# A rebuilt front of an expert layer: the gate turned round, the sort done with bf16 flags, three of four normalisations on GpSimd

## What is computed

```python
def _L0_ffn_ref(x, Wg, bg, W1, b1, W2, b2):     # x: the normalised rows
    x_flat = x.reshape(N * T, d)
    logits = x_flat @ Wg + bg
    probs = jax.nn.softmax(logits, axis=-1)
    assignments = jnp.argmax(probs, axis=-1)
    h = jnp.einsum('nd,edh->neh', x_flat, W1) + b1[None]
    h = jax.nn.gelu(h, approximate=False)
    eo = jnp.einsum('neh,ehd->ned', h, W2) + b2[None]
    selected = jnp.take_along_axis(eo, assignments[:, None, None], axis=1)[:, 0, :]
    w = jnp.take_along_axis(probs, assignments[:, None], axis=1)
    out = (w * selected).reshape(N, T, d)
x = x + _L0_ffn_ref(_layernorm(x, axis=-1), ...)
```

## Time and profile before

| | us |
|---|---|
| median of 3 runs | 2192.9 (2190.82 to 2194.61) |
| the profiled execution, whole | 2189.86 |
| its span, first to last instruction | 2187.2 |

### The profile page before, as it was taken

One profiled execution on the slowest core, in us unless ns is written; L12 is line 12 of the kernel. 1 busy time (PEld: TensorE's weight loads), 2 busy tenths in 40 slices (PEclk: granted clock), 3 DMA queues, 4 the chain that ended last, 5 costly groups with the idle time before them and its releaser, 6 DMA issues. The chain is left out here.

```text
span 2187.2 us, 34853 instructions
## 1 busy us (share of the span) xinstructions
PE 1982.6 (91%) x10933; PEld 1395.2 (64%) x10933; DVE 1400.2 (64%) x2902; ACT 1150.3 (53%) x2171; POOL 989.6 (45%) x1035
## 2 busy tenths in 40 slices
PE   4899999999999838899999999999999587799997
PEld 3667666677666425556565656565655286688896
DVE  4666657666565435767676767676766234688886
ACT  3555555455555422555555555555554243378785
POOL 2356555555564641444444444444444211255544
PEclk9999999999999768999999999999999855899999
DMA  5334353443434243333333334343423256222220
GB/s 154 88 92 130 104 143 104 121 136 94 135 100 104 87 164 83 73 88 102 92 102 93 102 93 102 93 102 93 102 69 88 88 187 230 58 85 80 87 85 24
DMA packets 129135, 227.27 MB, mean 104 GB/s; under 512 B 26362, under 2 KB 27426, under 8 KB 128992
## 3 DMA queue, kind: packets, MB, share of 16 engines
q1 hardware_dynamic: 110640, 194.97, 32.2%
q0 software_dynamic: 12704, 29.44, 4.9%
q10 hardware_dynamic: 5648, 1.07, 0.3%
HBM read 94.82 MB, written 37.24 MB: 60 GB/s over the span
## 5 line engine op out<-in xcount | busy, mean ns | idle before, releaser
L390 POOL TENSOR_TENSOR cross_probs<-cross_probs 128x1024 f32<-128x1024 f32 x128 | 305.2, 2388 | 361.4 <-ACT cross_probs L492 361.3
L590 DVE TENSOR_REDUCE cross_m_col<-cross_sS 128x1 f32<-128x512 f32 x512 | 340.1, 685 | 188.6 <-PE cross_sS L743 185.2
L492 ACT ACTIVATE cross_probs<-cross_sT 128x512 f32<-128x512 f32 x512 | 305.3, 598 | 266.9 <-PE cross_sT L759 261.9
L593 DVE CUSTOM_DVE_ANT_0 self_sS<-self_sS,self_tri 128x128 f32<-128x128 f32 (+3 forms) x512 | 248.9, 504 | 188.9 <-PE self_sS L743 185.7
L492 ACT ACTIVATE self_probs<-self_sT 128x256 f32<-128x256 f32 (+3 forms) x512 | 222.4, 438 | 245.5 <-PE self_sT L759 244.0
L378 POOL TENSOR_SCALAR_AFFINE_SELECT self_probs<-self_probs 128x256 f32<-128x256 f32 x256 | 105.6, 418 | 329.4 <-ACT self_probs L492 329.4
L743 PE MATMUL cross_sS<-cross_stack 97*128 97x512 f32 x512 | 211.1, 421 | 29.4 <-DVE cross_m_col L590 19.4
L759 PE MATMUL cross_sT<-cross_stack 98*128 98x512 f32 x512 | 212.8, 428 | 2.7 <-ACT cross_probs L492 2.7
L390 POOL TENSOR_TENSOR self_probs<-self_probs 128x512 f32<-128x512 f32 (+1 forms) x128 | 210.6, 1664 | 0.3 <-ACT self_probs L492 0.3
L759 PE MATMUL self_sT<-self_stack 98*128 98x256 f32 (+2 forms) x512 | 177.7, 360 | 2.4 <-ACT self_probs L492 2.4
L759 PEld LDWEIGHTS cross_sT<-cross_stack 98*128 98x128 f32 x512 | 94.3, 189 | 127.1 <-ACT cross_probs L492 79.9
(11 more groups left out here) (244 smaller groups left out, 4761.0 us busy)
## 6 DMA issues: line engine op xcount, KB each, us to landing
self_stack<-self_stage SPq DMA_DIRECT2D x384, 128.0 KB, 2.4
cross_stack<-cross_stage SPq DMA_DIRECT2D x288, 128.0 KB
self_rows<-in_x_dram SPq DMA_DIRECT2D x64, 256.0 KB, 3.4
moe_w<-in_L_ffn_W_dram SPq DMA_DIRECT2D x16, 1024.0 KB, 8.9
cross_stack<-cross_stage POOLq DMA_DIRECT2D x96, 128.0 KB, 3.3
x_after_self<-self_rows SPq DMA_DIRECT2D x32, 256.0 KB, 2.4
x_after_self_and_bias<-self_ahead SPq DMA_DIRECT2D x32, 256.0 KB, 2.1
cross_rows<-x_after_self SPq DMA_DIRECT2D x32, 256.0 KB, 4.3
```

Source lines behind the costliest of these rows:

```text
L390: pool.tensor_tensor(total, total, tile_of(n, kb)[:, js, q0:S], ALU.add).then_inc(added, 1)
L492: act.activation(tile_of(n, kb)[:, j, q0:S], sT[:, i % 2, q0:S], ACT.Exp, scale=SCALE).then_inc(exp_done, 1)
L590: dve.tensor_reduce(to, sS[:, k % 2], AX_X, ALU.max).then_inc(s_free, 1)
L593: dve.tensor_tensor_reduce(sS[:, k % 2, 0:width], sS[:, k % 2, 0:width], tri[:, S - P - qb * P:S - P - qb * P + width], 1.0, LOWEST, ALU.a ...
```

## The change

Only `expert_layer` changes, and the pitch of `x_after_cross`: its rows become 516 floats (`DX`), of which the last four hold a token's gate value, scale and shift.

- **Loads.** All 8 batches have buffers of their own, which lie where weights come later; SP issues the 8 loads at once. The three small loads go to ACT's queue. The weights of expert 3 are loaded last, after the sort, since its place is lent to the turned tiles and to the sort's tables.
- **Normalisation.** `ON_ACT = (0,)`: of a batch's 4 row tiles ACT normalises the first, POOL the others with a `tensor_scalar` (multiply, add; scale and shift one value for each partition). POOL also clears `rows` (128x3096) after batch 0.
- **Gate.** Now `wg`, padded to 32 columns, is stationary, and the turned tokens move, 128 columns; the four row tiles of a batch go to four groups of 32 output columns of the array. The product comes out turned; ACT copies it and one transpose turns it back. The product of batch b stands behind the first two turned row tiles of batch b+1.
- **Choice** of the expert: by pairs of batches (`choose(i)`, 128x64), the first three beside the gate stage. Gate values: four short pairs of operations (`weigh(i)`).
- **Places**: counts come from one narrow product for each half, and one product gives all ranks and totals; the scans on DVE are gone.
- **Records.** Gate value, scale and shift are not sorted but stored beside the rows by four DMAs of 16 bytes a token; the gather brings them. Only the token's number is sorted, as two bf16 numbers: `same_col` (DVE, 2 x 128x832), times the partition's number on ACT and times the tile's number on POOL, `at_row` in 4 pieces of 128x1024, then 32 products 104 wide.
- **Tile loop**: the same work. ACT's first three laps are written out, with a wait for each expert's weights; the factors are read from `rows`, not `cur`.

```diff
+        ON_ACT = (0,)
...
+            for b in range(B):
+                sp.dma_start(gx[b], x_batches[b][:, :, 0:D]).then_inc(loaded[b], 16)
...
+            for e in [e for e in range(E) if e != LENT] + [LENT]:
+                if e < NB:
+                    sp.wait_ge(loaded[weight_sem[e]], 16)
+                if e == LENT:
+                    sp.wait_ge(placed, 4)
+                load_weights(e)
...
-            with pool.Fori(0, B // 2) as pair:
-                for half in range(2):
-                    layernorm_scale(2 * pair + half, half)
-
-
-            pool.wait_ge(experts_ready, 1)
-            pool.memset(rows[:], 0.0).then_inc(rows_set, 1)
...
+                for t in range(NB):
+                    if t not in ON_ACT:
+                        pool.tensor_scalar(gx[b][:, t], gx[b][:, t], rec_tok[:, NB * b + t, 1:2],
+                                           rec_tok[:, NB * b + t, 2:3], ALU.mult, ALU.add).then_inc(g_norm[1], 1)
+
+            layernorm(0)
+            pool.wait_ge(route, 4)
+            for c in range(2):
+                pool.affine_select(out=carry[:, c, 0:NT], in_=carry[:, c, 0:NT], compare_op=ALU.is_ge, fill=0.0,
+                                   base=-1 - P * c, pattern=[[E, NT], [0, E]], channel_multiplier=-1)
+            pool.memset(rows[:], 0.0).then_inc(const_step, 1)
+            for b in range(1, B):
+                layernorm(b)
+
+            for half in range(2):
+                ts = slice(HALF * half, HALF * (half + 1))
+                pool.wait_ge(same_ready, half + 1)
+                pool.tensor_tensor(at_col[:, ts, 1], same_col[:, ts], t_no[:, ts].unsqueeze(2).broadcast_to([P, HALF, COLS]),
+                                   ALU.mult).then_inc(col_ready[1], 1)
+            pool.wait_ge(rec_stored, 16 * PAIRS)
+            pool.wait_ge(ids_ready, 1)
...
+            act.dma_start(b1_rows, b1.rearrange("e (k p) -> (e k) p", p=P)).then_inc(const_loaded, 16)
...
+            def store_rec(i):
+                ts = slice(EACH * i, EACH * (i + 1))
+                act.wait_ge(w_ready, i + 1)
+                with nc.allow_non_contiguous_dma("16 bytes beside each row, once"):
+                    act.dma_start(x_in.rearrange("b (t p) d -> p (b t) d", p=P)[:, ts, D:DX], rec_tok[:, ts]).then_inc(rec_stored, 16)
...
+            for b in range(B):
+                take_turned(b, 0)
+                take_turned(b, 1)
+                if b + 1 < B:
+                    normalize_batch(b + 1)
+                if b >= 1:
+                    take_gate(b - 1)
+                take_turned(b, 2)
+                take_turned(b, 3)
...
+            for half in range(2):
+                ts = slice(HALF * half, HALF * (half + 1))
+                dve.tensor_tensor(same_col[:, ts], col_no.unsqueeze(1).broadcast_to([P, HALF, COLS]),
+                                  col_i[:, ts].unsqueeze(2).broadcast_to([P, HALF, COLS]), ALU.is_equal).then_inc(same_ready, 1)
+            for c in range(NT // CHUNK):
+                ts = slice(CHUNK * c, CHUNK * (c + 1))
+                dve.tensor_tensor(at_row[:, ts], row_no.unsqueeze(1).broadcast_to([P, CHUNK, P]),
+                                  row_i[:, ts].unsqueeze(2).broadcast_to([P, CHUNK, P]), ALU.is_equal).then_inc(same_ready, 1)
...
-                for k in range(KT):
-                    op = pe.matmul(lg[half][:, t], gxT[t % 2][:, k * P:(k + 1) * P], wg[:, k],
-                                   start=k == 0, stop=k == KT - 1)
...
+                for k in range(KT):
+                    for t in range(NB):
+                        op = pe.matmul(gate_bank[b % 2][HD * t:HD * (t + 1)], wg[:, k],
+                                       turned[NB * (b % 2) + t][:, k * P:(k + 1) * P], start=k == 0, stop=k == KT - 1)
```

More of the change, by code:

```diff
@@ L904, in expert_layer @@
+        pos = take(NT * E).rearrange("p (t e) -> p t e", e=E)
+        over = take(E * LEVELS).rearrange("p (e m) -> p e m", e=E)
+        share = take(E * E).rearrange("p (e f) -> p e f", f=E)
+        tiles_of, start, ends = take(E), take(E), take(E)
+        top, first, total = take(NT), take(NT), take(NT)
+        place_i, col_i, row_i = take(NT, I32), take(NT, I32), take(NT, I32)
+        past = take((TILES + 1) * E).rearrange("p (t e) -> p t e", e=E)
+        te_f = take(TILES + 1)
         pT = ps("pT", [P, 2, D])
@@ L1078, in _ @@
-            act.wait_ge(less_ready, 1)
-            act.activation(expd, less, ACT.Exp).then_inc(exp_ready, 1)
+            act.dma_start(b1_rows, b1.rearrange("e (k p) -> (e k) p", p=P)).then_inc(const_loaded, 16)
+            with nc.allow_non_contiguous_dma("the gate's weights, rows of 32 bytes, once"):
+                act.dma_start(wg[:, :, 0:E], Wg.rearrange("(k p) e -> p k e", p=P)).then_inc(const_loaded, 16)
+            act.dma_start(bg_rows, bg.partition_broadcast(P)).then_inc(const_loaded, 16)
@@ new lines, in _ @@
+            dve.wait_ge(const_step, 13)
+            step(dve.tensor_copy(numbers, numbers_i))
+            step(dve.tensor_reduce(same, ident[:].rearrange("p (a e) -> p e a", e=E), AX_X, ALU.add))
+            stepped()
+            step(dve.memset(level[:, 0:1], -1.0))
+            step(dve.tensor_copy(carry[:].rearrange("p c t e -> p (c t) e"), over_tiles(same, 2 * (NT + 1))))
+            dve.wait_ge(const_loaded, 16 * 3)
+            for b in range(B):
+                row_stats(b)
+                if b in (5, 7):
+                    choose(b // 2 - 2)
@@ new lines, in _ @@
+            pe.wait_ge(const_step, 12)
+            pe.wait_ge(const_loaded, 16 * 3)
+            pe.transpose(b1_bank, b1_rows, ident[0:E * KT, 0:E * KT])
+            for b in range(B):
+                turn(b, 0)
+                turn(b, 1)
+                if b >= 1:
+                    gate(b - 1)
+                turn(b, 2)
+                turn(b, 3)
+                if b >= 1:
+                    turn_back(b - 1)
+            gate(B - 1)
+            turn_back(B - 1)
+            pe.wait_ge(const_step, N_CONST)
```

596 lines of the change are left out of this document (299 added, 297 removed).

## The result

| | before | changed kernel |
|---|---|---|
| median | 2192.5 us (4 runs, 2190.8 to 2194.6) | 2132.2 us (4 runs, 2127.6 to 2136.3) |
| ratio | | 0.9724, 95% interval 0.9701 to 0.9747 |
| profiled execution, whole | 2189.86 us | 2130.73 us |
| its span | 2187.2 us | 2128.9 us |

A forecast was written before the change was run, and what follows sets the result against it. TensorE's short instructions bound the gate stage, a DVE chain the routing, TensorE the unchanged tile loop. -4.5 - 31.9 - 18.0 + 2 = -52.4 us gave 2140.5, say 2141 us; own range 2134 to 2149, with two rivals 2124 to 2158.

The forecast's parts named there:

- Start: First issue of the expert layer to first statistic: small loads on ACT's queue land sooner, 6.0 us against 10.5, -4.5 us.
- Gate stage: First statistic to last addition of the bias: TensorE needs 5.6 us a batch, 55.8 us against 87.7, -31.9 us.
- A: Gate stage, the forecast itself: TensorE stays at 1.2 GHz and 5.6 us a batch, total 2141 us; chance 50%.
- B: Gate stage: TensorE's clock rises and POOL's 4.0 us a batch binds, stage 41.3 us, total about 2129; chance 25%.
- T: Gate stage: time of POOL's new `tensor_scalar` on 128x512, which no row showed; chosen as 0.68 us.
- Routing and sort: After the gate stage: last choice, gate values, places, tables and last products take 19.7 us against 37.7, -18.0 us.
- Small stores hidden: Four stores of 16 bytes a token before the first gather end near 17 to 19 us, under the sort's 19.7; cost nothing.
- rival D: Before the first gather: small stores end late, at twice the price, some 9 to 12 us more, about 2151; chance 8%.
- Gather, +2: First gather: shares the DMA engines with expert 3's weights and gets longer than 8.8 us by 2 (bounds 0 and 5).
- C: Gate stage: POOL's `tensor_scalar` costs the 2.34 us of its only row, 26.3 us more, total 2167; chance 9%.
- E: Gate product: the four groups of 32 columns run one after another, 40 us more, total 2181; chance 4%.
- F: Gate stage: POOL passes over the data for each of two operations; 83 us more at T = 4.7, total 2224; chance 4%.

The follow-up runs named there:

- statistics-first run: Changed kernel with VectorE waiting for the three small loads only before its first choice of experts, not before the first statistic: 2126.4 us.
- quarter-product run: Changed kernel with three of the four parts of the gate's product left out, transposes kept: 2132.6 us in one execution, gate stage 43.9 us.
- early clearing: Changed kernel with GpSimd's clearing of `rows` moved ahead of batch 0: 2128.7 us against 2128.2, gate stage 42.59 us against 45.21.
- combined run: Changed kernel with clearing before batch 0, statistics before the small loads, two of four normalisations on ScalarE, sort's multiplication on VectorE: 2120.4 us.

## Why the prediction was right, and where its steps were not

- **What bounds.** That all must come from between 1740 and 1890, and that the loop moves as a block, held: its 302.0 us became 301.9.
- **Start, -4.5 forecast, -0.6 measured.** The failed step is the landing of the small loads. I took 5.4 us for it from the earlier trace rows; here 8 MB were asked for at once, and the last took 8.9. That the 8 MB made the difference is likely, and not tested. The bound of 10.5 was the right one to fear. The statistics-first run shows the other 4.5 us still lying there.
- **Gate stage, -31.9 forecast, -42.5 measured.** At 1.2 GHz TensorE's pieces were right: 8 transposes 1.9 and the product 1.9 (forecast 1.78 and 1.8). What failed was the choice between A and B, the clock. I gave B 25% since the row of before shows 0.50 at a busy share of 99%; I read it as "short matmuls and transposes don't raise the clock", while it was the mix with the 8-column product that didn't: batch 0 and the quarter-product run show that the transposes do. By the rule on transposes the sum had stood at 55.8.
- **B's own sum, 41.3, measured 45.2.** T was 0.77, not 0.68: 0.3 in batch 0 and 1.3 over seven batches. The hold-up was 3.8, not 3.6. The tail behind GpSimd's last normalisation, which I had at 2.9, is 5.0 (1794.3 to 1799.4): transposes, copy, product, copy, turn back, each waiting for the last. Together these are the 3.9. That the clock would rise late, for which I had added 2 to 3 us to B's total, cost nothing, since GpSimd was behind anyway; the early clearing showed it.
- **Routing and sort, -18.0 forecast, -20.9 measured** (16.8 instead of 19.7). To the tables it took 5.9 and not 7.2, the tables 9.3 and not 10.8. That the two engines take turns was right. Too high was GpSimd's price, 1.97 for each multiplication where about 1.4 is left when the waits are taken off its 2.4; VectorE's six tables take 6.6 alone, not 6.9. In the forecast's sum, 1.12 ns for an element gives 0.93 and 1.15 us, not the 1.03 and 1.22 written there; the 0.1 more has no row, though 1.02 and 1.22 is what was measured.
- **Small stores hidden.** They were in the changed kernel, where GpSimd's wait was ended by VectorE's numbers. But the step looked only at their landing. That their issue holds ScalarE, with half of the sort behind it, wasn't in it, and in the combined run this is what binds the numbers; behind them GpSimd waits 2.8 us more for the landing, which is rival D itself.
- **Gather, +2.** Measured 2.0. Moving the weights, and the loads of `b2` behind them, took 4.1 off, so the shared DMA engines can well be its cause; which of the two loads made the 2 is open.
- **Rivals C, E and F** fell with the trace: T is a third of C's 2.34; 32 records took 1.94 us, so the four groups of columns do run side by side.
- The range of 2124 to 2158 held the result since it took in B's lower end; A's own range, 2134 to 2149, missed it. That the forecast came within 9 us is in part luck: the gate stage and the sort were 13.5 us faster than written, the small loads 3.9 slower, and the layer began 3.7 later by chance.

## What to carry to other kernels

A low clock beside a busy share of 99% says that this mix of instructions doesn't raise it; before one reads it as a property of one kind among them, see which of them fills the time. Once an engine has become the bound, balance its work against the others by their start-to-start times, which the overlap of records makes shorter than the sum of durations, and take one-off work out of its loop. A record can hold a wait: where two engines take turns, the durations of both are too long to be added. And a DMA costs twice on a busy machine: its landing, and its issue on the engine that sends it, with all that stands behind it there.

## What the runs showed of the hardware

- A stretch of which four fifths were 128-column transposes brought TensorE's clock to 2.4 GHz and held it there; the same transposes with products of 8 moving columns between them did so only for short stretches (mean 0.56). Batch 0's 16 transposes, with no product yet, were enough in eight of thirteen traces.
- Four matmuls of 32 output columns each, in four column groups, run side by side: 32 records of 128 moving columns took 1.94 us at 1.2 GHz and 1.08 at 2.4.
- A two-input operation of VectorE and a multiplication on GpSimd take turns: row tables of 1.22 us became 2.60 beside it, each ending 1.08 us after GpSimd's.
- GpSimd's `tensor_scalar` with two operations and one value per partition takes 0.77 us for 128x512 fp32, no more than ScalarE's 0.81; its power on 4 elements takes 1.0.
- The issue of four stores of 1024 pieces of 16 bytes each took ScalarE the longer, the earlier it fell into the bulk of the loads (386 GB/s): begun 46 to 47 us after the layer's first issue 12.0 to 12.1 us, at 52.9 us 10.4, at 54.3 us 9.9, at 56.0 us 8.4, at 57 to 58 us 6.4 to 7.6, at 61.5 us 3.7, and at 95.8 us 2.3.
